# Macaron block on one core: gated products of the two mixture layers moved into the ends of the loops before them

## The reference, cut to what matters

```python
x = x + 0.5 * ffn(layernorm(x), ...)
x = x + attn(layernorm(x), ...)
x = x + 0.5 * ffn(layernorm(x), ...)

def ffn(x):                                   # 8 experts, 2 per token, H = 176
    scores = softmax(x @ gate_w)
    topk_w, topk_idx = top_k(scores, 2)
    comb = zeros(T, 8).at[rows, topk_idx].add(topk_w)
    g = silu(einsum('td,edh->teh', x, w_gate)) * einsum('td,edh->teh', x, w_up)
    routed = einsum('teh,ehd,te->td', g, w_down, comb)
    shared = silu(x @ sw_gate) * (x @ sw_up) @ sw_down      # hidden width 352
    return routed + shared

def attn(x):                                  # 16 heads of 128, one key and value head
    qi, ki = hadamard(x @ wq_idx), hadamard(x @ wk_idx)
    I = sum over h of (x @ w_iw)[h] * relu(qi[h] @ ki.T)    # causal, per sequence of 256
    keep the 32 best keys of every token, softmax over them, o @ wo
```

## Time and profile before

| | us |
|---|---|
| median of 3 runs | 909.57 |
| lowest and highest of them | 906.76, 910.72 |
| the profiled execution | 902.63 |
| span of the profiled execution, first to last instruction | 900.8 |
| PE busy in that span | 874.1 |
| DVE busy | 673.9 |
| ACT busy | 553.0 |
| POOL busy | 392.4 |

### The profile page before, as it was taken

One profiled execution on the slowest core, in us unless ns is written; L12 is line 12 of the kernel. 1 busy time (PEld: TensorE's weight loads), 2 busy tenths in 40 slices (PEclk: granted clock), 3 DMA queues, 4 the chain that ended last, 5 costly groups with the idle time before them and its releaser, 6 DMA issues.

```text
span 900.8 us, 18966 instructions
## 1 busy us (share of the span) xinstructions
PE 874.1 (97%) x5779; PEld 784.6 (87%) x5779; DVE 673.9 (75%) x2359; ACT 553.0 (61%) x1605; POOL 392.4 (44%) x534
## 2 busy tenths in 40 slices
PE   9999999999998999999999999999999998999997
PEld 4778898888887899998999988999999996889996
DVE  6787669588897897776787767878587675757786
ACT  6765555467665767766667675667467674435562
POOL 0577787200002343342243343555258684316672
PEclk9999999999999999999999999999899999999999
DMA  9256984640000110000000005993001044524474
GB/s 347 95 167 241 358 311 146 133 85 12 1 1 1 36 36 25 24 1 1 2 1 1 1 1 152 317 304 89 1 1 48 25 162 155 228 73 135 134 250 169
DMA packets 52449, 96.23 MB, mean 107 GB/s; under 512 B 5824, under 2 KB 37184, under 8 KB 50304
## 3 DMA queue, kind: packets, MB, share of 16 engines
q1 hardware_dynamic: 44672, 73.20, 25.2%
q0 software_dynamic: 7680, 21.83, 7.7%
HBM read 44.99 MB, written 50.02 MB: 105 GB/s over the span
## 4 chain that ended last, share of the span: by engine, by line
PE 89%; DVE 6%; ACT 3%; issue 2%; POOL 0%; DVEq 0%; ACTq 0%; POOLq 0%
PE ps L825 43%; PE ps L830 37%; PE ps L1086 4%; PE ps L991 2%; PE ps L962 2%; DVE RR L1350 1%; PE ps L868 1%; ACT RR L1129 1%; ACT SP L1319 1%; DVE PA L1745 1%; DVE RA L1350 0%; POOL SP L1911 0%; DVE X L1638 0%; DVE SP L1784 0%; DVE X L1350 0%
## 5 line engine op out<-in xcount | busy, mean ns | idle before, releaser
L1911 POOL TENSOR_SCALAR SP<-SP,RC 128x128 f32<-128x128 f32 (+1 forms) x256 | 192.4, 768 | 252.0 <-DVE RC L1794 251.8
L1350 DVE TENSOR_TENSOR RR<-ps,RR 128x256 fp32r<-128x256 f32 (+2 forms) x322 | 157.7, 525 | 73.6 <-ACT RR L1129 72.5
L830 PE MATMUL ps<-RR,RA 128*128 (+1 forms) x894 | 162.8, 319 | 8.1 <-DVE RA L1350 4.8
L1129 ACT ACTIVATE RR<-ps 128x256 fp32r<-128x256 f32 (+2 forms) x322 | 137.3, 469 | 29.8 <-PE ps L825 27.7
L1319 ACT ACTIVATE SP<-SP,NB 128x128 f32<-128x128 f32 (+1 forms) x256 | 113.5, 444 | 66.9 <-DVE NB L1784 66.6
L830 PEld LDWEIGHTS ps<-RR,RA 128*128 128x128 f32 x894 | 129.7, 189 | 14.2 <-issue 13.2
L825 PE MATMUL ps<-xh,RR 128*128 128x512 f32 x368 | 133.6, 407 | 0.3 <-DVE PA L1350 0.3
L830 PE MATMUL ps<-RR 128*128 128x256 f32 x768 | 103.9, 285 | 3.0 <-DVE RR L1350 3.0
L1745 DVE SCALAR_TENSOR_TENSOR PA<-R,IW,PA 128x128 f32<-128x128 f32 x240 | 84.6, 414 | 29.6 <-ACT R L1311 29.4
L1879 POOL DMA_INDIRECT yr<-FA,IDX x78 | 84.3, 1081 | 47.5 <-DVE FA L1672 17.8
L830 PEld LDWEIGHTS ps<-RR 128*128 128x128 f32 x768 | 97.1, 192 | 4.0 <-DVE RR L1350 3.6
(11 more groups left out here) (252 smaller groups left out, 1886.2 us busy)
## 6 DMA issues: line engine op xcount, KB each, us to landing
xg<-stage SPq DMA_DIRECT2D x15, 1161.0 KB, 14.5
FA<-xg SPq DMA_DIRECT2D x78, 129.0 KB, 2.9
kept<-RR SPq DMA_DIRECT2D x8, 1216.0 KB, 6.0
RR<-kept SPq DMA_DIRECT2D x8, 1216.0 KB, 12.4
X<-yr POOLq DMA_DIRECT2D x6, 512.0 KB, 5.4
RAW<-yr SPq DMA_DIRECT2D x6, 512.0 KB, 5.3
RAW<-wex_in SPq DMA_DIRECT2D x8, 352.0 KB, 8.1
RAW<-wsh_in SPq DMA_DIRECT2D x6, 384.0 KB, 7.4
```

The source lines that it names most:

```text
L830: return e.matmul(o, a, c, start=start, stop=stop, skip_group_check=True)
L1129: return e.activation(o, i, ACT.Copy)
L1350: return e.tensor_tensor(o, p, q, alu)
L1911: ins = e.tensor_scalar(SP[:, k, i, o:o + w], SP[:, k, i, o:o + w], RC[:, k, 2 * i + z:2 * i + z + 1], None, ALU.mult)
```

## The change

It alters the order in the list and what such an order needs in waits and buffers. The matmuls are the same but for 10 warm ones.

1. Head. `warm` has 30 matmuls instead of 40. Group 0 is centred first, half by DVE and half by ACT, then group 1 by DVE, and group 0 is turned first. The first `gu` is written in two halves (`gu` the gate, `gv` the other factor), with both `unturn` stages between them, which now write into one bank and are read by DVE with one pair of instructions (`untwist`) instead of two. Groups 3 and 2 are also centred half by each engine, and `down` 1 stands ahead of the turn of group 3. The statistics of group 3 are split in two. The addition to X is a stage of its own, `deposit`.
2. POOL. The second address comes from a table, so `tag` is one instruction instead of two. The IDX computations are stages of their own (`index`); 0 and 1 of the first layer stand ahead of the last four scatters. The tag of group 2 stands behind the first round of group 3.
3. Openings of the loops. `turn_x` 0 and 1 of the first layer stand ahead of the last two `down` stages; in the second layer 0 stands ahead of the last `down`, and 1 behind it and behind `deposit`. In the second layer both splits wait for those downs, since their buffers overlap. The last two `lift` copies are one step later.
4. End of the first loop. Two of the three `gu` of group 2 are written into steps 38 and 39 of the loop.
5. End of the attention. The four halves of the first two `gu` of the second layer stand between `wo` 61, 62 and 63: one half before each, one before `wo` 62 besides, and one behind `wo` 63.
6. End of the second loop. One of the three `gu` of group 3 is written into step 38.

```diff
+APART = ((0, 0, 0), (1, 0, 0), (1, 0, 1))
...
     def sparse(n, fills):
-        yield ("turn_x", n, 0)
-        yield ("turn_x", n, 1)
...
-                yield ("turn_x", n, j + 2)
+                yield from [("turn_x", n, j + 2), ("index", n, j + 2)]
...
-    yield from [("warm", 40), ("tokens",)]
+    yield from [("warm", 30), ("tokens",)]
...
-    yield from high(("sh", 0, 0)) + [("moments", "m0", 0, 8, 0)] + centre("m0", 1, 4, "dve") + centre("m0", 0, 0, "act")
-    yield from low(("sh", 0, 0)) + [("flip", "m0", 1, 4, 5), ("flip", "m0", 0, 6, 7)] + high(("sh", 0, 1))
+    yield from high(("sh", 0, 0)) + [("moments", "m0", 0, 8, 0)] + centre("m0", 0, 0, "dve", "act") + centre("m0", 1, 4, "dve")
+    yield from [("flip", "m0", 0, 4, 5), ("flip", "m0", 1, 6, 7)] + low(("sh", 0, 0)) + high(("sh", 0, 1))
...
+    yield from low(("sh", 0, 1), ("sh", 0, 2)) + [("gu", 0, 0, 0), ("stats", "m0", 12, 2, 12), ("means", 2)]
+    yield from [("unturn", 0, 0, 1), ("unturn", 0, 1, 1), ("untwist", 0, 0, 1), ("pick", 0, 0), ("gv", 0, 0, 0)]
...
+    yield from part_of("tm", 2) + centre("m0", 3, 12, "dve", "act") + centre("m0", 2, 8, "dve", "act")
+    yield from part_of("down", 1) + [("flip", "m0", 3, 6, 7)] + part_of("tm", 3) + high(parts[0])
...
+    yield from spread(0, 2, 0) + spread(0, 3, 0) + [("tag", 0, 2)] + spread(0, 2, 1) + [("index", 0, 0), ("index", 0, 1)]
+    yield from [("tag", 0, 3)] + spread(0, 3, 1) + high(*parts[4:6]) + part_of("gu", 5) + [("tables", 0), ("tail", 0)]
...
+    yield from [("turn_x", 0, 0), ("turn_x", 0, 1)] + part_of("down", 7) + low(*parts[11:14]) + lifts(*parts[10:14])
+    yield from part_of("down", 8) + [("deposit", 0, 3)] + prefetch(0)
...
         if j == 0:
-            yield from low(*parts[14:16]) + lifts(*parts[14:16])
+            yield from low(*parts[14:16])
+        if j == 1:
+            yield from lifts(*parts[14:16])
...
+        elif j == 38:
+            yield ("gu", 0, 2, 0)
+        elif j == 39:
+            yield from [("gu", 0, 2, 1), ("tm", 0, 2, 0)]
...
-    yield from shared(0, [2], fill3)
+    yield from (st for st in shared(0, [2], fill3, 2) if st != ("tm", 0, 2, 0))
...
-    yield from [("wo", 61), ("pv", 62), ("flip_p", 63), ("wo", 62), ("pv", 63), ("wo", 63)]
+    yield from [("gu", 1, 0, 0), ("wo", 61), ("pv", 62), ("flip_p", 63), ("gv", 1, 0, 0), ("wo", 62), ("pv", 63)]
+    yield from [("gu", 1, 0, 1), ("wo", 63), ("gv", 1, 0, 1)]
...
-            yield from prefetch(1)
-
-    yield from shared(1, [0, 1, 2], fill4, 0, between4)
+            yield from prefetch(1) + [("turn_x", 1, 0), ("index", 1, 0)]
+        elif (s, late) == (10, 1):
+            yield from [("turn_x", 1, 1), ("index", 1, 1)]
+
+    yield from shared(1, [0, 1, 2], fill4, 2, between4)
...
+        elif j == 38:
+            yield ("gu", 1, 3, 0)
         elif j == 39:
-            yield ("store", 0, 0)
+            yield from [("store", 0, 0), ("tm", 1, 3, 0)]
...
-    yield from shared(1, [3], fill6)
+    yield from (st for st in shared(1, [3], fill6, 1) if st != ("tm", 1, 3, 0))
...
                 elif kind == "turn_x":
...
-                    if j == 0:
+                    if j < 2 and m:
                         t.wait_ge(S["down"], n["down"])
...
                 elif kind == "tag":
...
-                    then(e.tensor_copy(rows[:, :, D], W2[:, 1, 4 * g:4 * g + 4]))
-                    then(e.tensor_scalar(rows[:, :, D + 1], token[:, 4 * g:4 * g + 4], float(T), None, ALU.add))
+                    then(e.tensor_copy(rows[:, :, D:DW], TAGS[:, 1, 4 * g:4 * g + 4, :]))
```

More of the change, by code:

```diff
@@ L118, in order @@
-    yield from low(("sh", 0, 1), ("sh", 0, 2)) + part_of("gu", 0) + [("stats", "m0", 12, 4, 12), ("means", 2)]
-    yield from [("unturn", 0, 1, 1), ("unturn", 0, 0, 3), ("pick", 0, 0)] + part_of("gu", 1) + part_of("tm", 0)
-    yield from [("sel", 0, 0), ("shift", 0, 0)] + part_of("gu", 2) + [("squares", 2)] + part_of("tm", 1)
-    yield from [("raise", 0, 0), ("count", 0, 0, 6), ("place", 0, 0, 6), ("choose", 0, 0)] + marks(0, 0, 1) + scatters(0, 0, 1)
-    yield from [("root", 1, 8, 8)] + part_of("down", 0) + part_of("gu", 3) + [("moments", "m0", 8, 8, 8)]
@@ new lines, in order @@
+    yield from [("unturn", 0, 0, 1), ("unturn", 0, 1, 1), ("untwist", 0, 0, 1), ("pick", 0, 0), ("gv", 0, 0, 0)]
+    yield from part_of("gu", 1) + part_of("tm", 0) + [("sel", 0, 0), ("shift", 0, 0)] + part_of("gu", 2) + [("squares", 2)]
+    yield from part_of("tm", 1) + [("raise", 0, 0), ("stats", "m0", 14, 2, 14)]
+    yield from [("count", 0, 0, 6), ("place", 0, 0, 6), ("choose", 0, 0)] + marks(0, 0, 1) + scatters(0, 0, 1)
+    yield from [("root", 1, 8, 8)] + part_of("down", 0) + part_of("gu", 3) + [("moments", "m0", 8, 8, 8)]
@@ L498, in tally @@
             n["read", st[3]] = (n["read", st[3]] or ()) + ((st[4], n["xn", st[4]]),)
-        if kind == "down" and st[3] == 2 or kind == "sum":
-            n["xres"] += 2 if kind == "down" else 1
-            if kind == "down":
+        if kind in ("deposit", "sum"):
+            n["xres"] += 2 if kind == "deposit" else 1
+            if kind == "deposit":
                 n["emptied", 4], n["emptied", 5] = n["xres"] - 1, n["xres"]
@@ L770, in macaron_kernel @@
         GU = [st for st in stages if st[0] == "gu"]
+        UP = [("gv", *st[1:]) if st[1:] in APART else st for st in GU]
         TURNS = {}
@@ L774, in macaron_kernel @@
                 TURNS.setdefault(st[1:3], []).extend((st, bank) for bank in banks(st))
-        LOGITS = {st[1:3]: st for st in stages if st[0] == ("logits" if st[1:2] == (1,) else "unturn")}
+        LOGITS = {st[1:3]: st for st in stages if st[0] == "logits" and st[1] == 1}
+        LOGITS.update({(0, g): st for st in stages if st[0] == "untwist" for g in BATCHES[0][st[2]]})
         WIDE = {st[2]: st for st in stages if st[0] == "logits" and st[1] == 0}
@@ L928, in _ @@
                     t.wait_ge(*lo_of(("sh", m, i)))
-                    for z in range(2):
+                    for z in {"gu": (0,), "gv": (1,)}[kind] if a in APART else range(2):
                         bank = 2 * z + c % 2
@@ L1451, in _ @@
                         tt(L[:, dc, :], PS[bank][:, :], f(H[:, dc, :]), ALU.subtract).then_inc(S[f"bank{bank}"], 1)
-                elif kind == "unturn" or kind == "logits" and a[0] == 1:
-                    m, g, bank = a
-                    t.wait_ge(S["gate"], n.get("logits", 0) + 1 if m else n.get("unturn", 0) + 1)
-                    if m:
-                        t.wait_ge(S["lgp"], 128)
-                        t.wait_ge(S["bias"], 16)
-                        t.wait_ge(S["weights"], 2)
+                elif kind == "untwist":
+                    m, q, bank = a
+                    r = span(m, q)
+                    t.wait_ge(S["gate"], n["unturn"])
+                    two = PS[bank][:, 0:128].rearrange("p (t k e) -> p t k e", k=2, e=NE)
+                    after(own[0])
+                    c = then(e.tensor_copy(LG[:, r, :], two[:, :, 0, :]))
+                    after(c)
+                    tt(LG[:, r, :], LG[:, r, :], two[:, :, 1, :], ALU.add).then_inc(S[f"bank{bank}"], 1)
+                elif kind == "logits" and a[0] == 1:
+                    m, g, bank = a
+                    t.wait_ge(S["gate"], n.get("logits", 0) + 1)
+                    t.wait_ge(S["lgp"], 128)
+                    t.wait_ge(S["bias"], 16)
+                    t.wait_ge(S["weights"], 2)
                     two = PS[bank][:, 0:64].rearrange("p (t k e) -> p t k e", k=2, e=NE)
-                    t.wait_ge(S["dve"], own[0])
+                    after(own[0])
                     c = then(e.tensor_copy(LG[:, 4 * g:4 * g + 4, :], two[:, :, 0, :]))
@@ L1630, in _ @@
                        ALU.subtract).then_inc(S["gl"], 1)
[L1631 to L1633 removed]
+                elif kind == "deposit":
+                    m, g = a
+                    t.wait_ge(S["down"], n["down"])
                     for b in range(2):
```

49 lines of the change are left out of this document (25 added, 24 removed).

## The result

| | before | after |
|---|---|---|
| median of 14 runs each, the same chip (us) | 907.37 | 910.75 |
| lowest and highest | 905.67, 910.72 | 908.69, 915.96 |
| ratio, with its 95% interval | | 1.0035 (1.0021 to 1.005) |
| the profiled execution of the changed kernel | | 910.81, span 909.0 |

The forecast was 4.7 us less; measured are 3.4 us more. That is a real loss, still inside the 0.5% that were called no change, but outside the range (910.0) by 0.8. That range was laid around a median of 909.57; measured against 907.37, its upper end stood for a loss of 0.4, and the miss is 3.0.

A forecast was written before the change was run, and what follows sets the result against it. PE was taken as the bound, busy 874.1 of 900.8 us. Terms -2.2 -2.2 -2.4 +1.2 +1.6 -1.1 +0.4 = -4.7 took the median from 909.57 to 904.9; own range 903.9 to 906.0, whole range 901.5 to 910.0.

The forecast's parts named there:

- The base: Sum made against the profiled 902.63 us, 6.94 below the timed median 909.57; the difference carried over to the median unchanged.
- The head: Kernel start: fewer warm matmuls, earlier first turn, covered waits at the first gu and group 3's turn; 2.2 us won.
- The opening of the first loop: First expert loop's start: hidden 0 no longer waits (1.5), turn_g 1 waits less (0.7); together 2.2 us won.
- the rival of the transfers: First loop: transfers set its pace, 4.4 us given back and up to 3.5 added, total 912.8; chance 0.08.
- The end of the first loop: Drain: two gu cover waits and keep the clock up (4.0), less a new wait of 1.5 to 1.6; net 2.4 won.
- the rival with two falls: Clock falls behind the first loop's end too (1.6 more), and longer at the second layer's start (1.0 more): 907.5; chance 0.24.
- The end of the attention: Waits ahead of wo 61 to 63 vanish, but group 3's turn waits 5.25 us: 1.2 lost, plus 1.6 by the clock.
- the rival "no fall": Clock stays up behind the 5.25 us wait, or the drain keeps its 4.0; total 903.3; chance 0.20.
- The opening of the second loop: Second expert loop's start: hidden 0 starts at once instead of waiting 1.36, hidden 1 waits some 0.5; 1.1 us won.
- the end of the kernel: Last sink stages and the routed rows' read come later, so DVE's last sums wait; 0.4 us lost.

The follow-up runs named there:

- before_third: The kernel before, without an edit, run for a third trace; 903.1 us, ratio 1.001 to before.
- after_fourth: The changed kernel without an edit, run again; 902.55 us, ratio 1.0012 to before.
- best_again: The changed kernel with the end of the attention and the end of the second loop put back as before; 899.52 us, ratio 0.9979 to before.
- before_again: The kernel before, without an edit, run for a second trace; 909.41 us, ratio 0.9992 to before.
- after_again: The changed kernel without an edit, run for a second trace; 911.97 us, ratio 1.0029 to before.
- head_only: The changed kernel with only the new head and first opening kept, parts 3 (second layer), 4, 5 and 6 undone; 910.71 us, ratio 1.0019 to before.
- after_third: The changed kernel without an edit, on a chip without the head's waits; 903.57 us, ratio 1.0011 to before.
- old_att_drain: The changed kernel with the end of the attention and the end of the first loop as before; 899.84 us, ratio 0.9981 to before.
- old_att_tail: The changed kernel with the end of the attention and the end of the second loop as before; 899.08 us, ratio 0.9979 to before.
- old_att: The changed kernel with the end of the attention alone put back as before; 899.53 us, ratio 0.9968 to before.
- filled: The changed kernel with 12 + 12 gated products of the next slices put ahead of the turn of group 3; 903.33 us, ratio 1.0015 to before.
- filled_old_tail: The same as filled, with the end of the second loop as before; 902.92 us, ratio 1.0007 to before.

## Why the forecast was wrong, step by step

The three traces of one chip, without waits in the head, cut at the same places in each (stage lengths in us, worked out from the start times of the instructions named):

| from, to | `before_third` | `after_fourth` | `best_again` |
|---|---|---|---|
| start, POOL's first scatter | 30.09 | 28.20 | 28.12 |
| to the silu of tile 0 | 38.33 | 37.96 | 37.94 |
| to the silu of tile 36 | 80.89 | 79.54 | 79.33 |
| to the attention's first exponential | 134.15 | 133.55 | 133.40 |
| to PE's transposes of unit 62, ahead of `wo` 61 | 463.44 | 464.41 | 464.50 |
| to the 21st silu of shared products | 49.17 | 52.01 | 49.27 |
| to the 2nd tile's silu, second loop | 10.24 | 9.22 | 9.21 |
| to the 65th silu of this kind | 48.04 | 47.91 | 48.02 |
| to the end | 47.35 | 47.40 | 47.11 |

**The base.** The step "I take the difference in time over to the median unchanged" carried the plan over from an execution that has no waits in the head to runs which most likely have them: on the chip of `before_again` and `after_again` both kernels do, and so does the trace of the changed kernel shown first. With these waits the stage from first scatter to tile 0's silu took 46.5 to 49.3 us (56.98 in `head_only`) instead of 38, and a gain in the head can be swallowed there. It alone explains little of the sign, since on the chips without them the change brought +0.0011 and +0.0012, nearest +1 us and not -4.7. What the 2 us more are in the two comparisons with the waits (1.0035 and 1.0029) stays open; the waits alone differ by more than that between traces.

**The head: half as much.** The steps themselves came. Timeline of PE in `after_fourth`, and of POOL:

```profile
10.70 1.06 PE L890 MATMUL ps<-ident,PA 128*128 128x128 f32 x8 [0.70 <-DVE PA L1459]
...
28.20 1.18 POOL L1899 DMA_INDIRECT xg<-PA,XI  x1 [18.14 <-DVE xn L1638]
...
33.06 1.16 PE L890 MATMUL ps<-ident,XN 128*128 128x128 f32 x8 [1.07 <-DVE RT L1373]
38.48 0.42 PE L914 MATMUL ps<-ident,stage 16*128 16x16 f32 x4 [0.33 <-ACT stage L1152]
...
61.07 0.63 PE L985 MATMUL ps<-ident,FA 128*128 128x128 f32 x4 [0.30 <-ACT FA L1244]
...
64.80 1.32 PE L852 MATMUL ps<-RR,RA 128*128 x6
```

The first turn is at 10.70 (forecast 10.9) and the first scatter 1.9 us earlier. But the turn of group 2 waits 1.07 for DVE to read the banks of group 3's turn. `down` 1, which stood between the two turns, now stands ahead of both; I had taken its move as covering the turn of group 3 (the 0.39 of the earlier trace rows, which are gone) and never asked what stands behind it. The silus of the shared slices ahead of that turn come 1.7 to 2.1 us earlier than in `before_third`, those behind it only 0.8 to 1.3, where the head was to give 2.2.

**The opening of the first loop: as forecast.** `hidden` 0 starts at 64.80 without a wait. In `before_third` it stood at:

```profile
67.16 1.23 PE L830 MATMUL ps<-RR,RA 128*128 x6 [1.36 <-DVE RA L1350]
```

That is 2.36 earlier, where 62.8 was forecast: the 1.36 of the wait and the 1.0 left of the head. The second half of this step shows behind tile 0: the 0.96 that PE waited ahead of `turn_g` 1 in `before_third` is gone, and the silu of tile 4 comes 3.1 us earlier than there (74.30 against 77.40). Of the 4.4 forecast for head and opening 3.1 came, and what is missing is the head's. In the table this second half counts in the row to tile 36.

Whether the loop keeps it is not clear. From the silu of tile 4 to that of tile 36 it took 70.00, 70.03 and 71.91 in the three traces of the kernel before, 71.40 in `after_fourth` and 72.02 in `after_third`. Where the waits in the head delay the loop's start, the kernels with the changed order take 68.2 to 69.8 there. So part of a lead may be taken back in the loop, as the rival of the transfers has it; no run tests this. PE's waits for a fetch in the loop are 0.21 in all in `after_fourth`.

**The end of the first loop: 2.4 forecast, 0.5 to 1.2 found.** The 1.69 in `before_third` is gone, and the wait ahead of the attention's turn is 1.50 (forecast 1.5 to 1.6). Behind it the clock stays up, so the rival with two falls is out as well. Up to that turn the gain is there: it starts 13.87 us behind the silu of tile 36, against 16.63 in the trace of before and 15.12 in `before_third`. But it isn't kept. Behind the turn PE waits at two places that I hadn't looked at:

```profile
159.57 1.06 PE L890 MATMUL ps<-ident,xn 128*128 128x128 f32 x8 [1.50 <-ACT xn L1189]
...
165.53 0.74 PE L852 MATMUL ps<-RR,RA 128*128 128x256 f32 x4 [0.66 <-DVE RA L1373]
...
175.32 0.50 PE L847 MATMUL ps<-xh,RT 128*128 128x512 f32 x1 [1.60 <-DVE X L1670]
```

The last is for DVE's addition to X, 1.28 in `before_third`. DVE does it right behind the split of a weight, for which ACT waits for the weight's transfer. Timelines of ACT and DVE of `after_fourth`, then of ACT of `before_third`:

```profile
172.71 0.63 ACT L1152 ACTIVATE RR<-stage 128x512 fp32r<-128x512 f32 x1 [5.94 <-DMA stage<-wo_in]
...
173.37 0.69 DVE L1373 TENSOR_TENSOR RR<-stage,RR 128x512 fp32r<-128x512 f32 x1 [5.65 <-ACT RR L1152]
...
176.56 0.63 ACT L1129 ACTIVATE RR<-stage 128x512 fp32r<-128x512 f32 x1 [3.17 <-DMA stage<-wo_in]
```

So an earlier turn mostly lengthens the wait for this chain. The 2 us of half clock in the earlier trace rows went the same way, and they aren't a fixed price of the wait of 1.72 either: `before_third` has nearly the same wait and full clock behind it.

```profile
158.12 0.62 PE L830 MATMUL ps<-RR,RA 128*128 x3 [1.69 <-DVE RA L1350]
...
158.00:160.00 2.00, 1.88 (x11) 1.66 (x12) 1.76 (x9) 0.75 (x2) 0.93 (x1) 1.00 0.50 176
```

Its turn comes 1.5 earlier for that, but from tile 36 to the first exponential it takes 134.15, against 134.22 in the trace of before and 134.40 in `before_again`, which both have the half clock and no wait for X. What the half clock cost the kernel is thus 0.1 to 0.3. The term counted time that PE lost at one place as time of the kernel. With this end undone (`old_att_drain` against `old_att_tail`) the stage is 133.27 against 133.01, and the medians, which hold the end of the kernel too, are 899.84 and 899.08: 0 to 0.8.

**The attention itself.** All kernels but the one before take 1.0 to 1.2 us more from its first exponential to the transposes of unit 62, where the half-clock stretch near 640 is as long. It is no wait at one place: up to unit 42, ahead of that stretch, the start of each unit's transposes falls behind that in `before_third` little by little, by 0.66 in `after_fourth`, 0.71 in `best_again` and 0.79 in `head_only`. It was no term of the sum. Its cause is open; the attention's own order is the same in these kernels.

**The end of the attention: mechanism and size as forecast.** No waits are left ahead of `wo` 61 to 63. `wo` 63 starts at 754.35, the turn at 762.55, 8.20 behind it (forecast 8.19), and PE waits:

```profile
762.55 1.94 PE L890 MATMUL ps<-ident,FA 128*128 128x128 f32 x8 [5.12 <-DVE FA L1459]
...
764.00:766.00 2.00, 2.00 (x8) 1.61 (x7) 2.00 (x4) 1.44 (x3) 0.00 (x0) 0.50 1.02 429
...
743.66:795.67 52.01, 46.33 (x272) 39.82 (x273) 31.46 (x104) 19.50 (x35) 15.81 (x19) 0.93 0.41 156
```

The last row spans the stage of the table; the same of `before_third`, with waits of 0.76, 0.76, 1.41 and 1.05 where the earlier trace rows have 0.80, 0.76, 1.41 and 1.03:

```profile
746.90:796.07 49.17, 44.65 (x272) 38.14 (x273) 31.38 (x104) 19.23 (x35) 15.99 (x20) 1.00 0.43 163
```

Idle 4.52 before, 5.68 after: 1.2 lost, as forecast. PE's busy time grows from 44.65 to 46.33, 1.7 us for as many matmuls (forecast 1.6). Together 2.8, and 3.1 in `after_third` (52.30). The stage must begin ahead of `wo` 61; the texts on record that give 44.8 and 48.1 for it begin at POOL's 53rd scatter, behind the first of the three waits, and so make the loss look larger by 0.3. In all nine traces with the old end of the attention the stage takes 49.2 to 49.3, in the seven with the changed one 52.0 to 52.5, with the waits in the head or without them. The clock stood at 0.50 behind the wait of 5.12 in all these seven, so the rival "no fall" is out, and the rule of the Trainium skill that the prediction named (TensorE: Matmul & The Clock Gate, "Why this matters for your kernels") holds here. That 1.6 came so near is partly luck: its price came from the stretch of the earlier trace rows, whose loss was gone again by the first exponential.

**The opening of the second loop** gave 1.0 (forecast 1.1) and **the end of the kernel** cost 0 to 0.6 (forecast 0.4): DVE's last sums now wait for the read, which the earlier trace rows had ready in time. Timelines of POOL, SP and DVE of the changed kernel:

```profile
894.92 1.01 POOL L1913 DMA_INDIRECT yr<-FA,IDX  x1 [0.32 <-issue]
...
897.54 0.80 SPq L2033 DMA_DIRECT2D RAW<-yr  x2
...
903.47 1.23 DVE L1373 TENSOR_TENSOR X<-X,RAW 128x1024 f32<-128x1024 f32 x1 [0.24 <-DMA RAW<-yr]
```

**The sum of what was found** on that chip is -3.1 (head and opening, to tile 4) -0.5 (rest of the first loop) -0.6 (its end) +1.0 (attention) +2.8 (its end) -1.0 (second opening) -0.1 +0.1 = -1.4; the spans are 900.2 and 901.7. The timed runs of the same kernel there say 1.0012, +1.1 us. A trace is one execution, and these two differ from others of the same kernels: with 70.00 for the loop behind tile 4, as in the trace of before, and not 71.91, the sum is +0.5. The half-clock stretch near 640, which takes 3.4 us in some traces of both kernels and 6.8 in others, makes another 1.5 us. Against the forecast of -4.7, the steps that failed are that of the head (1.2 short, since a turn lost its cover) and that of the first loop's end (1.8 short: won on PE and lost again to a chain behind it), and 1.0 came on top in the attention, for which the sum had no term. The loss at the attention's end was forecast and came. None of the rivals was it as it stands; that of the transfers may hold a part.

## What to carry to other kernels

Work that is moved into small waits pays only if the long chain behind them doesn't need it: here 24 products covered most of a chain of 8.2 us, and spending 18 of them on waits of 3.0 us in all turned four spread waits into one of 5.12, with half clock behind it. For each step that is moved, ask what stood between its old neighbours, as well as what it now covers: the turn of group 2 lost its cover of `down` 1 in this way. And follow a gain to the next wait behind it: at the end of the first loop PE was 0.9 to 2.9 us earlier at the turn, and 0.5 to 1.2 of it was left at the first exponential. And before pricing anything, hold the profiled execution against the timed ones; if it lies outside their spread, take a second trace of the same kernel, since a stall or a low clock that one execution has may be missing in the next.

## What the runs showed of the hardware

- **Waits without a releaser.** On the chip of `before_again`, and in the trace of the changed kernel shown first, every trace, of either kernel, has idle times of 1 to 7 us on PE, ACT and DVE that nothing in the program is seen to release, most between 38 and 59 us from the start, in some kernels up to 80. The first of them repeat closely (PE at 40.2 to 40.3 for 2.10, 2.15 and 2.14 in the three traces with the new head), the later ones don't. On three other chips no trace has them. The median of the kernel before was 907.37 and 910.39 where they stand and 901.58 to 901.79 on the others, 0.6 to 1.0% apart. That the scatters cause them was not tested, since the test fell on chips without them. The cause is open.
- **Spread waits kept the clock in these traces, bunched ones didn't.** In `old_att` PE waits 0.81, 0.76, 1.41 and 1.05 over 17 us and stays at 1.00; `filled` waits as much in that stage (3.96 us), but bunched, with PE busy for 1.40 of 4.00 us, and drops. A single wait of 1.69 to 1.72 us was followed by half clock in two traces of the kernel before and not in the third. Timeline of PE and busy times of `old_att`:

```profile
746.96 1.21 PE L851 MATMUL ps<-RR 128*128 128x256 f32 x8 [0.81 <-DVE RR L1372]
...
763.48 0.74 PE L889 MATMUL ps<-ident,FA 128*128 128x128 f32 x5 [1.05 <-DVE FA L1458]
...
764.00:768.00 4.00, 4.00 (x26) 3.49 (x24) 3.06 (x5) 2.75 (x6) 0.00 (x0) 1.00 1.02 429
```

- **The length of a low stretch is not a constant of the program.** With the same instructions ahead of it, it was 3.4 us in `filled_old_tail` (768.3 to 771.7) and 10.2 in `filled` (769 to 779), which made 2.6 us of difference.
- **PE's time at half clock is not always the kernel's.** At the end of the first loop a stretch of 3.4 us made the attention's turn 1.5 to 1.6 us later and its first exponential only 0.1 to 0.3; a wait of 1.28 us that stands between them at full clock was gone.
